# Gate and up products of an expert layer: high and low rows side by side against the high weights, 24 matmuls a unit in place of 36

## What is computed

```python
x = x + _L0_xattn_ref(_layernorm(x), ctx_2048, mask)
...
# feed-forward: 64 experts, 8 for each token, some rerouted by similarity
gu = lax.ragged_dot(xs, jnp.swapaxes(gate_up_proj, 1, 2), group_sizes)
gate, up = jnp.split(gu, 2, axis=-1)          # 192 columns each
hact = jax.nn.silu(gate) * up
y = lax.ragged_dot(hact, jnp.swapaxes(down_proj, 1, 2), group_sizes)
out = jnp.zeros_like(x).at[tok].add(y * w[:, None])
```

## Time and profile before

| | us |
|---|---|
| median of 3 runs (lowest, highest) | 810.89 (810.79, 812.53) |
| the profiled execution: time / span | 809.93 / 808.1 |
| PE busy, DVE busy, ACT busy, POOL busy | 678.4, 554.3, 453.6, 518.3 |
| wide units (W over 256), 17 of them | 216.42 to 385.71 |
| W = 256, 17 units | 385.71 to 527.07 |
| W = 224, 16 units | 527.07 to 659.90 |
| W = 192, 12 units | 659.90 to 754.24 |
| W = 160 and what is left over | 754.24 to 808.1 |

### The profile page before, as it was taken

How to read it: one execution, slowest core, us unless ns; L and a number is a source line. 1 busy time by engine, 2 the same in 40 slices (tenths; PEclk the granted TensorE clock), 3 DMA queues, 4 the chain that set the end, 5 groups by cost and what they waited for, 6 DMA issues and landing times. The chain is left out here.

```text
span 808.1 us, 15268 instructions
## 1 busy us (share of the span) xinstructions
PE 678.4 (84%) x4278; PEld 560.5 (69%) x4278; DVE 554.3 (69%) x1308; ACT 453.6 (56%) x885; POOL 518.3 (64%) x461
## 2 busy tenths in 40 slices
PE   4999999731599999999999998989898998999730
PEld 2555555420489999888988888878787887888630
DVE  5699999962277666777677677676767776767620
ACT  3544554210266666666775766767666676666620
POOL 6037777776638887887766666676657666666440
PEclk9999999955599999999999999999999999999965
DMA  8999896605659999999999999999999999999467
GB/s 281 373 369 336 292 312 232 206 18 161 171 153 221 241 234 242 237 239 257 244 270 254 272 243 245 258 234 260 241 252 222 252 236 240 237 248 242 92 124 159
DMA packets 107557, 189.93 MB, mean 235 GB/s; under 512 B 33521, under 2 KB 35441, under 8 KB 106065
## 3 DMA queue, kind: packets, MB, share of 16 engines
q1 hardware_dynamic: 74274, 125.61, 50.7%
q0 software_dynamic: 33200, 63.35, 38.1%
HBM read 143.40 MB, written 56.24 MB: 247 GB/s over the span
## 5 line engine op out<-in xcount | busy, mean ns | idle before, releaser
L1224 PE MATMUL bank<-xh,w1h 128*128 128x256 f32 (+7 forms) x768 | 228.8, 298 | 18.3 <-DVE h L897 18.2
L1226 PE MATMUL bank<-xh,w1l 128*128 128x256 f32 (+7 forms) x768 | 220.4, 287 | 0.0
L1225 PE MATMUL bank<-xl,w1h 128*128 128x256 f32 (+7 forms) x768 | 220.4, 287 | 0.0
L610 POOL DMA_INDIRECT xg<-normed_tokens,list x145 | 158.2, 1091 | 54.1 <-issue 48.2
L1224 PEld LDWEIGHTS bank<-xh,w1h 128*128 128x128 f32 x768 | 147.2, 192 | 23.4 <-issue 23.2
L619 POOL DMA_INDIRECT out_rows<-ys,list x73 | 115.8, 1587 | 70.9 <-ACT ys L1041 58.1
L594 POOL DMA_INDIRECT list_table<-token,slot x112 | 114.4, 1022 | 69.8 <-DVE token L765 36.6
L619 POOL DMA_INDIRECT second_sum<-ys,list x70 | 113.3, 1618 | 66.4 <-ACT ys L1041 45.5
L913 DVE TENSOR_TENSOR xl<-bank,xh 128x448 fp32r<-128x448 f32 (+3 forms) x145 | 84.2, 616 | 97.3 <-ACT xh L1048 96.3
L1225 PEld LDWEIGHTS bank<-xl,w1h 128*128 128x128 f32 x768 | 147.7, 192 | 0.0
L1226 PEld LDWEIGHTS bank<-xh,w1l 128*128 128x128 f32 x768 | 147.5, 192 | 0.0
(11 more groups left out here) (210 smaller groups left out, 1104.4 us busy)
## 6 DMA issues: line engine op xcount, KB each, us to landing
raw<-in_w SPq DMA_DIRECT2D x195, 256.0 KB, 4.7
raw<-in_w2a SPq DMA_DIRECT2D x65, 256.0 KB, 4.5
ctxT_s<-in_ctxT SPq DMA_DIRECT2D x16, 768.0 KB, 8.4
ctx_s<-in_ctx SPq DMA_DIRECT2D x16, 768.0 KB, 8.1
raw<-in_w2b SPq DMA_DIRECT2D x65, 128.0 KB, 5.8
list_table<-blank SPq DMA_DIRECT2D x30, 256.0 KB, 6.7
x_in<-in_x SPq DMA_DIRECT2D x16, 224.0 KB, 7.9
out_rows<-x SPq DMA_DIRECT2D x16, 224.0 KB, 6.6
```

The source lines that it names most:

```text
L610: pool.indirect_dma_start(xg[u.on(XGS)][0:u.m, t, :], None, normed, bass.IndirectOffsetOnAxis(ap=lists[u.on(LISTS)][0:u.m, t, 0:1], axis=0 ...
L1224: pe.matmul(bank[m][:, 0:W], wh, mh, start=(c == 0), stop=False)
L1225: pe.matmul(bank[m][:, 0:W], wh, ml, start=False, stop=False)
L1226: mm = pe.matmul(bank[m][:, 0:W], wl, mh, start=False, stop=(c == DK - 1))
```

## The change

Units of at most 256 rows (`paired`: 46 of the 63, and the leftover loop) have `xh` and `xl` in one tile `xhl`. One matmul with the high weights goes over high and low rows together, 2W columns, and writes the high product into the first half of the PSUM bank and the low one into the second. The product with the low weights is added to the first half, as before. So a block takes 4 x 2 matmuls in place of 4 x 3, and a unit 24 in place of 36. The halves have to be added afterwards:

- bank 0: DVE sums the halves into `gs` (`sum_gate`), ACT takes silu from there;
- bank 1: ACT copies the second half to `uc`, DVE adds the first half to it into `us`, and waits for its own result before the multiply;
- bank 2: DVE sums the halves into `rs` (`sum_rest`); silu_rest and h_rest read it.

The four buffers lie in the memory of `blank`, a tile that only the first phase uses.

```diff
+PAIR = 256
...
+        self.paired = self.rows <= PAIR
...
-        xh = two("xh", [P, DK, WIDE], F32R)
-        xl = two("xl", [P, DK, WIDE], F32R)
+        xhl = two("xhl", [P, 2, DK, WIDE], F32R)
+        xh, xl = [t[:, 0] for t in xhl], [t[:, 1] for t in xhl]
+        spare = blank[:].rearrange("p n c -> p (n c)").bitcast(F32)
+        gs, us, rs, uc = [spare[:, i * PAIR:(i + 1) * PAIR] for i in range(4)]
...
+            def both(m, W):
+                return bank[m][:, 0:2 * W].rearrange("p (v w) -> p w v", v=2)
+            def sum_gate(u):
+                if u.paired:
+                    dve.wait_ge(gu_ps, u.n * 3 + 1)
+                    wait(dve, silu_s, u.n * 2)
+                    v.tensor_reduce(gs[:, 0:u.rows], both(0, u.rows), AX, ALU.add).then_inc(sum_s, 1)
+            def sum_rest(u):
+                if u.paired:
+                    dve.wait_ge(gu_ps, u.n * 3 + 3)
+                    wait(dve, h_s, u.n * 3)
+                    v.tensor_reduce(rs[:, 0:u.rows], both(2, u.rows), AX, ALU.add).then_inc(sum_s, 1)
             def h_gate(u):
                 W = u.rows
+                up = bank[1][:, 0:W]
+                if u.paired:
+                    dve.wait_ge(uc_s, u.pair + 1)
+                    wait(dve, h_s, u.n * 3)
+                    v.tensor_tensor(us[:, 0:W], bank[1][:, 0:W], uc[:, 0:W], ALU.add).then_inc(sum_s, 1)
+                    dve.wait_ge(sum_s, u.pair * 3 + 2)
+                    up = us[:, 0:W]
...
-                v.tensor_tensor(h[:, 0, 0:W], sg[:, 0, 0:W], bank[1][:, 0:W], ALU.mult).then_inc(h_s, 1)
+                v.tensor_tensor(h[:, 0, 0:W], sg[:, 0, 0:W], up, ALU.mult).then_inc(h_s, 1)
...
+                stage(sum_gate, r)
                 stage(h_gate, r)
                 early_stage(x_low, r + 1, (2,))
+                stage(sum_rest, r)
                 stage(w2_low, r)
...
             def silu_gate(u):
+                if u.paired:
+                    act.wait_ge(sum_s, u.pair * 3 + 1)
+                    a.activation(sg[:, 0, 0:W], gs[:, 0:W], ACT.Silu).then_inc(silu_s, 1)
+                    act.wait_ge(gu_ps, u.n * 3 + 2)
+                    a.copy(uc[:, 0:W], bank[1][:, W:2 * W]).then_inc(uc_s, 1)
...
             def silu_rest(u):
+                if u.paired:
+                    act.wait_ge(sum_s, u.pair * 3 + 3)
+                    a.activation(sg[0:FR, 1, 0:W], rs[0:FR, 0:W], ACT.Silu).then_inc(silu_s, 1)
...
-                for c in range(DK):
+                for c in range(DK if u.paired else 0):
+                    wh, wl = w1h[b][:, c, m * P:(m + 1) * P], w1l[b][:, c, m * P:(m + 1) * P]
+                    halves = bank[m][:, 0:2 * W].rearrange("p (v w) -> p v w", v=2)
+                    pe.matmul(halves, wh, xhl[b][:, :, c, 0:W], start=(c == 0), stop=False)
+                    mm = pe.matmul(bank[m][:, 0:W], wl, xh[b][:, c, 0:W], start=False, stop=(c == DK - 1))
+                for c in range(0 if u.paired else DK):
```

More of the change, by code:

```diff
@@ L111, in __init__ @@
         self.tile = TILES_BEFORE[n]
+        self.paired = self.rows <= PAIR
+        pairs = sum(1 for nt, m in RANKED[:n] if nt * m <= PAIR)
+        self.pair = pairs if g is None else g + pairs
     def on(self, ring):
@@ L296, in program @@
         xT_ps = sem("xT_ps"); gu_ps = sem("gu_ps"); y_ps = sem("y_ps")
-        xh_s = sem("xh_s"); xl_s = sem("xl_s"); silu_s = sem("silu_s"); h_s = sem("h_s")
+        sum_s = sem("sum_s"); uc_s = sem("uc_s"); xh_s = sem("xh_s"); xl_s = sem("xl_s"); silu_s = sem("silu_s"); h_s = sem("h_s")
         hh_s = sem("hh_s"); hl_s = sem("hl_s"); ys_s = sem("ys_s")
@@ L895, in h_rest @@
                 dve.wait_ge(gu_ps, u.n * 3 + 3)
-                v.tensor_tensor(h[0:FR, 1, 0:W], sg[0:FR, 1, 0:W], bank[2][FR:P, 0:W], ALU.mult).then_inc(h_s, 1)
-                v.tensor_tensor(h[FR:P, 1, 0:W], sg[0:FR, 1, 0:W], bank[2][FR:P, 0:W], ALU.mult).then_inc(h_s, 1)
+                up = rs[FR:P, 0:W] if u.paired else bank[2][FR:P, 0:W]
+                v.tensor_tensor(h[0:FR, 1, 0:W], sg[0:FR, 1, 0:W], up, ALU.mult).then_inc(h_s, 1)
+                v.tensor_tensor(h[FR:P, 1, 0:W], sg[0:FR, 1, 0:W], up, ALU.mult).then_inc(h_s, 1)
             def h_low(u):
@@ L941, in late @@
             def late(u):
+                sum_gate(u)
                 h_gate(u)
+                sum_rest(u)
                 w2_low(u)
@@ L1017, in silu_gate @@
                 W = u.rows
-                act.wait_ge(gu_ps, u.n * 3 + 1)
                 wait(act, h_s, u.n * 3)
-                a.activation(sg[:, 0, 0:W], bank[0][:, 0:W], ACT.Silu).then_inc(silu_s, 1)
+                if u.paired:
[3 more added lines that the diff above has]
+                    a.copy(uc[:, 0:W], bank[1][:, W:2 * W]).then_inc(uc_s, 1)
+                else:
+                    act.wait_ge(gu_ps, u.n * 3 + 1)
+                    a.activation(sg[:, 0, 0:W], bank[0][:, 0:W], ACT.Silu).then_inc(silu_s, 1)
             def silu_rest(u):
                 W = u.rows
-                act.wait_ge(gu_ps, u.n * 3 + 3)
-                a.activation(sg[0:FR, 1, 0:W], bank[2][0:FR, 0:W], ACT.Silu).then_inc(silu_s, 1)
+                if u.paired:
+                    act.wait_ge(sum_s, u.pair * 3 + 3)
+                    a.activation(sg[0:FR, 1, 0:W], rs[0:FR, 0:W], ACT.Silu).then_inc(silu_s, 1)
+                else:
+                    act.wait_ge(gu_ps, u.n * 3 + 3)
+                    a.activation(sg[0:FR, 1, 0:W], bank[2][0:FR, 0:W], ACT.Silu).then_inc(silu_s, 1)
             def h_high(u):
```

## The result

The changed kernel is slower: 920.15 us median (918.91 to 920.65, 4 runs), against 811.71 (810.79 to 814.51, 4 runs) for the kernel before. The ratio is 1.134, 95% interval 1.131 to 1.137. Forecast was 916.3 in 890 to 958.

What follows compares the result with a forecast made beforehand. A ring of DVE and ACT steps, not TensorE, was taken as the bound. The insertion adds 105.4 us to the profiled 809.93, giving 915.3; with the median 0.96 above that, 916.3 us, range 890 to 958.

Steps and rivals of the forecast that it cites:

- The ring: DVE and ACT steps from one unit's hh cast to the next: 8.49 us at W = 256, becoming 10.99.
- TensorE time to spare: PE's own work in a W = 256 unit put at 7.6 of 8.49 us, leaving about 0.9 us.
- The insertion: Sums, silu, copy and addition added behind w1l: 1.44 + 0.47 + 0.59 = 2.50 us a unit at W = 256.
- the longer list of waits: Ahead of DVE's multiply for bank 1: some 0.02 us, part of the 0.47 us step.
- The stages were to grow: Insertion times units at W = 256, 224, 192 and 160: 42.5, 36.5, 24.6 and 1.8 us, together 105.4.
- The price of the reduction: DVE's sum of two halves costs by elements only: 0.68, 0.61 and 0.55 us at the three widths.
- The cheap end: Rival: a sum costs like any instruction with 256 outputs, 0.41 us; 891 us in all, 10%.
- the dear end: Rival: sums cost 10 ns per output, 2.6 us for 256; about 1120 us in all, 4%.
- What silu had for cover: silu_gate on ACT ran beside DVE's w1l at no cost; now it waits for bank 0's sum, after w1_low(r+1).
- The idle piece ahead of gate_up(r,0): PE waits for silu_rest about 3.1 us in one piece and does not hold the ring.
- The clock rival: TensorE's clock falls to 1.2 GHz; three quarters of a unit at it adds 1.1 us, 967 us in all; 12%.
- a granted clock well below 1: Sign that the prediction is wrong: TensorE's granted clock in the stages falls well below 1.

Runs made afterwards that it cites:

- e1: The kernel before with the changed kernel's 24 products and without the sums of the halves (high x low product left out in paired units): 810.54 us, ratio 1.0002.
- e2: The changed kernel with its sums, but with three products for each chunk again, 36 a unit: 920.21 us, ratio 1.135 to the kernel before.
- e4: The kernel before with two lines exchanged in DVE's order, h_rest(r) before w2_low(r): 787.65 us, ratio 0.970 to the kernel before.
- e3: The changed kernel with one line moved, DVE sums bank 0 before w1_low of the next unit: 856.92 us, ratio 1.057 to the kernel before.

## Why the prediction was right

**The ring was the bound, not TensorE.** Predicted 8.49 us with 0.9 us of TensorE time to spare. e1 and e2 show it from both sides: the products changed alone, with the sums or without, move nothing. PE's busy share of over 90% in the earlier trace rows was no evidence: it says how closely TensorE's work fitted into the ring, not what set the ring's length. The time to spare was rather 1.0 us or more, since e4 does all 36 products in a unit of 7.47 us.

**The insertion.** Predicted 1.44 + 0.47 + 0.59 = 2.50 us at W = 256, measured 1.49 + 0.46 + 0.61 = 2.56. The ring was put at 10.99 and is 11.04. The 0.02 us for the longer list of waits ahead of the multiply stood on no row; the step it is part of was put at 0.47 and measured 0.46. The stages were to grow by 42.5, 36.5, 24.6 and 1.8 us and grew by 44.0, 36.6, 26.6 and 2.8. The forecast of 916.3 was 4 us low. The three paired stages and the last were 4.5 us longer together than forecast, the first phase 1.0 longer and the wide stage 0.7 shorter; and the median, put 0.96 us above the profiled execution, stood level with it (920.15 and 920.16).

**The price of the reduction.** This was the disputed one. Groups of DVE by form, mean ns in the last but one column:

```profile
L896 DVE TENSOR_REDUCE blank<-bank 128x256 f32<-128x512 f32 x17 | 11.6, 684 | 0.0
...
L896 DVE TENSOR_REDUCE blank<-bank 128x224 f32<-128x448 f32 x16 | 9.9, 618 | 0.0
...
L896 DVE TENSOR_REDUCE blank<-bank 128x192 f32<-128x384 f32 x12 | 6.6, 550 | 0.0
```

0.684, 0.618 and 0.550 us where 0.68, 0.61 and 0.55 were predicted: elements count, outputs don't. The cheap end (0.41) and the dear end (2.6) of the range both fall. The estimate of 658 ns, worked out from VectorE: DVE Perf Modes of the Trainium skill (cycle table, section on the errata), is 4% low against the 684 measured. The page's warning against a reduction on a hot path, which stands in its section Rules for kernel authors, held here more for the path than for the reduction, as e3 shows.

**What silu had for cover.** The prediction named w1l as the work that hid silu_gate, and the written order as what takes it away. e3 gives the cover back and finds 63 us.

**TensorE in time.** The idle piece ahead of gate_up(r,0), predicted 3.1 us, is 3.08 in the unit shown, which has the full clock. Over all units the mean is 96.9/44 = 2.2 us, because at the lower clock TensorE's work fills part of it.

**The clock rival** was half right. The granted clock did fall, to a mean of 0.91, 0.89 and 0.86 in the three stages, which before was 0.99 or 1.00. If only the two levels 1.00 and 0.50 occur, TensorE was at the lower one for 18 to 28% of the time. But the units kept their pace. Here are the windows of two units of W = 256 in a row, each from one gate_up(r,0) to the next (columns as in the earlier trace rows):

```profile
483.13:494.18 11.05, 9.17 (x43) 7.70 (x43) 7.93 (x13) 6.25 (x11) 5.33 (x4) 0.85 0.75 198
494.18:505.22 11.04, 7.86 (x42) 6.38 (x43) 7.92 (x12) 6.25 (x11) 5.31 (x4) 1.00 0.74 192
```

The first has a clock of 0.85 and is 11.05 us long, the second has 1.00 and 11.04. The wait behind the first, at 494.18, is 1.88 us, behind the second 3.08. The fall ate idle time. So a granted clock well below 1, which the prediction named as a sign that it was wrong, came without the cost that the rival put on it: the rival needed three quarters at the lower level. The clock did cost at the end, where nothing covers it: the ten down products of the last of the 63 units, after a wait of 4.89 us,

```profile
873.83 0.72 PE L1285 MATMUL bank<-w2h,hh 128*80 128x512 f32 x1 [4.89 <-DVE hl L933]
...
877.75 0.63 PE L1290 MATMUL bank<-w2h,hl 128*80 128x512 f32 x1
```

start 3.92 us apart from first to last, at a granted clock of 0.50. In the kernel before, the same ten start 2.12 us apart (765.25 to 767.37), after a wait of 3.40 us. That is 1.8 us more, and from the first of them to the end of the trace it is 44.47 us against 42.85 before. This covers the 1.0 us by which the last stage was forecast too short.

**What was off.** The insertion was put 0.05 to 0.06 us too low at each width. From hh to hh in units away from a change of width the ring went from 8.49 to 11.04 us at W = 256, from 8.23 to 10.56 at 224 and from 7.96 to 10.07 at 192 (before: 732.77 to 740.73; after: 822.99 to 833.06). That is 2.55, 2.33 and 2.11 us where 2.50, 2.28 and 2.05 were predicted. At W = 192 DVE's steps bear it out: 1.25 from the first sum to the addition, 0.39 and 0.47, together 2.11.

The prediction also misread the ring at W = 192. The 7.88 us of the earlier trace rows are the last unit of its stage; the ten before it take 7.95 to 7.97 us. So ring and stage mean (7.86) don't agree to 0.02 us there, and the stage's growth of 26.56/12 = 2.21 us a unit is not the ring's. The stages are cut at PE's first matmul, whose distance from the ring differs at their ends; at W = 192 that makes up the 1.2 us beyond 12 x 2.11.

## What to carry to other kernels

When engines with a written order release each other, follow one unit through them by start times until you come back to where you began; if the steps add up to the unit's whole time, only these steps count, whatever the busy shares say. A saving outside the ring turns into waiting; an operation put into it costs its full length plus whatever it uncovers, unless it falls into time in which its engine waited anyway (the first sum in e3); and moving one line of the order can be worth more (23 to 25 us here) than a third of the gate and up matmuls. Look for what hides a cheap operation before you give it a new predecessor.

## What the hardware showed that was not expected

A matmul that reads two separate pieces of SBUF and writes the two halves of a bank cost no more than a plain one: a double and a single product of W = 256 took 0.35 us together, as three plain ones did. And TensorE's clock could fall for a fifth of a stage without any change in its pace: a unit with a granted clock of 0.85 took 11.05 us, the next one with 1.00 took 11.04.
